# Attention and routed experts on one core: the attention steps written out in a new order of units

## The reference

```python
x = L0_attn_x                                            # (4, 512, 128)
# attention: 16 heads of 8, causal; weights with a LoRA part
qkv = x @ w_attn.T + b_attn + 0.5 * (x @ la.T @ lb.T)
att = softmax(where(causal, q @ k.T / sqrt(8), -inf))
y   = lora_linear(att @ v, w_proj, b_proj, la_proj, lb_proj)
x   = layernorm(x + y)
# experts: 8 experts of width 352, the best two per token
probs = softmax(x @ router_w); w, idx = top_k(probs, 2); w /= sum(w)
x   = layernorm(x + sum_k w_k * (silu(x @ gate[idx_k]) * (x @ up[idx_k])) @ down[idx_k])
```

## Time and profile before

| | us |
|---|---|
| runs | 396.70, 397.21, 397.75 |
| profiled execution, its own time | 399.86 |
| span in that profile | 398.0 |
| start-up, to the first score for a row max | 0 to 34 |
| maxima of groups 0 and 1, then PE idle | 34 to 66.7 |
| attention steps 0 to 15 | 66.7 to 241.2 |
| last batch's rows, scatters, tables | 241.5 to 273.8 |
| experts (39 tiles) | 273.8 to 368 |
| gathering, second normalising, store | 368 to 398 |

### The profile page before, as it was taken

How to read it: one execution, slowest core, us unless ns; L and a number is a source line. 1 busy time by engine, 2 the same in 40 slices (tenths; PEclk the granted TensorE clock), 3 DMA queues, 4 the chain that set the end, 5 groups by cost and what they waited for, 6 DMA issues and landing times.

```text
span 398.0 us, 7773 instructions
## 1 busy us (share of the span) xinstructions
PE 276.3 (69%) x2334; PEld 155.7 (39%) x2335; DVE 215.8 (54%) x551; ACT 156.8 (39%) x258; POOL 158.9 (40%) x273
## 2 busy tenths in 40 slices
PE   3984602969787888788878774305999999999200
PEld 2542201323243334333334222203777777877100
DVE  1489901647578677887786002441655555555082
ACT  1371002647465477547654361110333233333014
POOL 8047100323325386448644700270233343444262
PEclk9996555689899699989996898555999999999755
DMA  6199998754500000000000100042021111110253
GB/s 155 48 232 193 358 202 274 193 78 77 86 3 3 9 30 23 3 0 30 30 3 1 50 8 0 0 155 60 25 60 53 48 48 48 53 49 28 84 145 103
DMA packets 36107, 30.31 MB, mean 76 GB/s; under 512 B 4130, under 2 KB 33989, under 8 KB 36054
## 3 DMA queue, kind: packets, MB, share of 16 engines
q1 hardware_dynamic: 27710, 20.59, 21.9%
q10 hardware_dynamic: 6000, 5.07, 5.3%
q0 software_dynamic: 2368, 4.27, 3.2%
HBM read 16.86 MB, written 13.09 MB: 75 GB/s over the span
## 4 chain that ended last, share of the span: by engine, by line
PE 45%; issue 10%; DVE 10%; POOL 8%; DMA 8%; ACTq 7%; ACT 6%; SPq 3%; another core or an unknown queue 2%; POOLq 1%; DVEq 0%
PE slot L1260 12%; PE pvo L1274 7%; ACTq L673 6%; PE pvo L1089 5%; DMA Qs<-mT 4%; PE slot L1266 3%; PE slot L1068 3%; ACT Pt L655 3%; POOL rows_scratch L527 3%; POOL Pt L503 2%; PE slot L1049 2%; SPq L352 2%; PE misc L1097 1%; PE misc L1253 1%
## 5 line engine op out<-in xcount | busy, mean ns | idle before, releaser
L788 DVE TENSOR_REDUCE negm<-slot 128x2 f32<-128x1024 f32 (+2 forms) x96 | 97.5, 1040 | 54.5 <-PE slot L1049 53.4
L655 ACT ACTIVATE Pt<-slot 128x1024 f32<-128x1024 f32 (+1 forms) x96 | 83.8, 881 | 72.6 <-PE slot L1068 64.5
L503 POOL TENSOR_SCALAR_AFFINE_SELECT Pt<-Pt 128x512 f32<-128x512 f32 x56 | 35.8, 639 | 88.2 <-ACT Pt L655 67.0
L571 POOL DMA_INDIRECT chosen_scratch<-Pt x39 | 38.3, 983 | 65.7 <-ACT Pt L713 64.4
L1068 PE MATMUL slot<-Qs,Ks 51*128 51x512 bf16 (+3 forms) x256 | 37.4, 331 | 31.5 <-DMA Qs<-mT 22.8
L1089 PE MATMUL pvo<-Pt,V 128*9 128x128 f32 (+3 forms) x512 | 55.6, 498 | 0.9 <-issue 0.9
L1260 PE MATMUL slot<-GUW,Pt 128*128 x156 | 55.0, 476 | 0.0
L942 DVE COPY Pt<-slot 128x256 f32<-128x256 f32 x39 | 16.6, 425 | 42.7 <-PE slot L1266 24.2
L1049 PE MATMUL slot<-Ks,Qs 48*128 48x512 bf16 (+3 forms) x256 | 39.0, 345 | 0.0
L527 POOL DMA_INDIRECT rows_scratch<-early,place x32 | 31.8, 994 | 15.4 <-issue 8.3
L1274 PE MATMUL pvo<-DW,Pt 128*128 (+1 forms) x234 | 33.4, 278 | 1.2 <-ACT Pt L713 0.7
(11 more groups left out here) (165 smaller groups left out, 373.6 us busy)
## 6 DMA issues: line engine op xcount, KB each, us to landing
Qs<-parts_scratch SPq DMA_DIRECT2D x8, 384.0 KB, 6.9
Ks<-parts_scratch SPq DMA_DIRECT2D x8, 384.0 KB, 9.4
Pt<-rows_scratch SPq DMA_DIRECT2D x39, 65.0 KB, 1.7
Qs<-chosen_scratch SPq DMA_DIRECT2D x8, 256.0 KB, 5.0
parts_scratch<-Pt SPq DMA_DIRECT2D x4, 384.0 KB, 5.5
parts_scratch<-early SPq DMA_DIRECT2D x4, 384.0 KB, 3.5
GUW<-in_L_ffn_gate_proj_dram ACTq DMA_DIRECT2D x1, 1408.0 KB, 16.6
GUW<-in_L_ffn_up_proj_dram ACTq DMA_DIRECT2D x1, 1408.0 KB, 18.1
```

The lines of the kernel that those rows point to most:

```text
L503: pool.affine_select(out=v, in_=v, compare_op=ALU.is_ge, fill=0.0, base=0, pattern=[[0, HQ], [1, P]], channel_multiplier=-1).then_inc(sele ...
L571: pool.indirect_dma_start(chosen_scratch, bass.IndirectOffsetOnAxis(xg[:, ring, C:C + 1].bitcast(U32), 0), ys[:, ring % OUT_RING, :], None ...
L655: act.activation(p_view(par, kb)[:, h0:h0 + heads, :].rearrange("p (c a) q -> p a c q", a=2), t_view(u, (2 * u + 1) % 3), ACT.Exp, scale=S ...
L788: dve.tensor_reduce(negm[:, par, qb, h0:h0 + heads].rearrange("p (c a) -> p a c", a=2), s_view(u, n), AX_X, ALU.max, negate=True).then_inc ...
```

## The change

The order of work on each engine is written out step by step, with the same arithmetic:

- the loops over the batches on DVE, ACT and POOL are gone, as are the semaphores that count inside them;
- PE's units come as q0 k0 q1 k1 q2 q3 k2 q4 k3 k4 k5 q5, with new slots to match, and the four groups of values of a step are placed anew;
- the maxima of a group are laid out so that one transpose of 48 columns does for four, and two DMAs for four bring them to the stacks;
- the end of a batch is spread over three steps: k = 1 (y, projection, residual, statistics, normalised rows), k = 2 (x1, router, choice), k = 3 (count, places);
- the normalised rows are made by ACT, as x times the inverse deviation plus a shift that DVE forms;
- POOL's scatters are at other places: the first at the end of step k = 3, three in the next step, four in the one after, three of these behind its last select;
- the expert weights are loaded by SyncE, one expert behind the maxima of each of groups 4 to 11.

```diff
-            def store_maxrows(g, par):
+            def store_maxrows(g):
 
                 sp.wait_ge(mT_copied, g + 1)
-                for h in range(HQ):
-                    row = HALF * (h % 2) + ROWS
-                    sp.dma_start(Qs[row:row + PARTS, bass.ds(g, 1), h // 2, :],
-                                 mT[PARTS * h:PARTS * (h + 1), par, :]).then_inc(maxrows[par], 16)
+                for a in range(2):
+                    row = HALF * a + ROWS
+                    n = MAX_ROWS // 2
+                    sp.dma_start(Qs[row:row + PARTS, g].rearrange("e c (t q) -> e (c t) q", q=P),
+                                 mT[n * a:n * (a + 1), g % 2, :]).then_inc(maxrows[g % 2], 16)
+
+            def load_expert(e):
+                for w, src in enumerate((gate_proj, up_proj)):
+                    sp.dma_start(GUW[:, e, w, :], src[e]).then_inc(experts_loaded, 16)
+                full = F // P
+                sp.dma_start(DW[:, e, 0:full, :], down_proj[e, 0:full * P, :].rearrange("(k p) c -> p k c", p=P)).then_inc(experts_loaded, 16)
+                sp.dma_start(DW[0:F - full * P, e, full, :], down_proj[e, full * P:F, :]).then_inc(experts_loaded, 16)
...
-            with sp.Fori(2, G // 2) as pair:
-                store_maxrows(2 * pair, 0)
-                store_maxrows(2 * pair + 1, 1)
+            for g in range(4, G):
+                store_maxrows(g)
+                if g < 4 + E:
+                    load_expert(g - 4)
...
+            def first_step(g):
+                b = g // 4 - 2
+                if b >= 0:
+                    scatter_rows(b, 1)
+                select(g, 0)
+                if b >= 0:
+                    scatter_rows(b, 2)
+                select(g, 1)
+                if b >= 0:
+                    scatter_rows(b, 3)
+                select(g, 2)
+                split_max(g + 2)
+                select(g, 3)
+
+            def second_step(g):
+                b = g // 4 - 2
+                if b >= 0:
+                    scatter_rows(b, 4)
+                select(g, 0)
+                if g >= 4:
+                    inverse_deviation(g // 4 - 1)
+                select(g, 1)
+                select(g, 2)
+                split_max(g + 2)
+                select(g, 3)
+                if b >= 0:
+                    for n in range(5, 2 * TB):
+                        scatter_rows(b, n)
+                if g >= 4:
+                    number_rows(g // 4 - 1)
...
+            def normed(b):
+                act.wait_ge(shift1_ready, b + 1)
+
+                act.wait_ge(scattered, 16 + 2 * TB * 16 * b)
+                for t in range(TB):
+                    last = act.activation(rows[:, 0, t, 0:C], XR[:, t, :], ACT.Identity, bias=shift1[:, t:t + 1], scale=rstd[:, t:t + 1])
+                last.then_inc(x1_ready, 1)
...
+            def step(g):
+                k, b = g % 4, g // 4 - 1
+                if k == 1 and b >= 0:
+                    copy_yT(b)
+                exp(g, 0)
+                if k == 2 and b >= 0:
+                    copy_x1(b)
+                exp(g, 1)
+                if g >= 1:
+                    copy_pv(g - 1)
+                if g + 1 < G:
+                    copy_mT(g + 1)
+                exp(g, 2)
+                if k == 2 and b >= 0:
+                    copy_scores(b)
+                exp(g, 3)
+                exp(g, 4)
+                exp(g, 5)
+                if k == 1 and b >= 0:
+                    normed(b)
+                if k == 2 and b >= 0:
+                    exp_gap(b)
...
+            def step(g):
+                k, b, scores = g % 4, g // 4 - 1, g + 2 < G
                 for u in range(NU):
+                    if u == NU - 1 and g >= 1:
+                        if k == 2 and b >= 0:
+                            choose(b)
+                        normalize(g - 1)
+                        if k == 1 and b >= 0:
+                            shift_mean(b)
                     if scores:
-                        row_max(g + 2, par, u, (2 * u) % 3)
+                        row_max(g + 2, u)
+                    if u == 2 and k == 1 and b >= 0:
+                        residual(b)
+                    if u == 3 and k == 1 and b >= 0:
+                        deviations(b)
+                    if u == 1 and k == 3 and b >= 0:
+                        place_rows(b)
...
+                scores_q(g + 2, 1)
+                if k == 2 and ended:
+                    pe.wait_ge(y_done, g - 1)
+                    transpose_x1(b)
...
+                pe.wait_ge(max_done, NU * (g + 2) + 2)
+                scores_q(g + 2, 3)
...
+                transpose_max(g + 1)
+                pe.wait_ge(exp_done, NU * g + 2)
+                scores_k(g, 2)
+                pe.wait_ge(max_done, NU * (g + 2) + 3)
+                scores_q(g + 2, 4)
+                if k == 2 and ended:
+                    pe.wait_ge(mT_copied, g + 2)
+                    route(b)
```

More of the change, by code:

```diff
@@ L527, in scatter_rows @@
                 pool.indirect_dma_start(rows_scratch, bass.IndirectOffsetOnAxis(place[:, j, t:t + 1], 0),
                                         rows[:, j, t, :], None).then_inc(scattered, 16)
-            def step(g, k, end=None, chosen_before=None, scores=True):
-                selects = not isinstance(g, int) or g < MASKED_FROM
-                par = k % 2
-                if end is not None:
-                    inverse_deviation(end)
-                for kb in range(TB):
-                    if selects:
-                        select(g, par, kb)
-                    if kb == 1 and end is not None:
-                        number_rows(end)
-                    if kb == TB - 1 and scores:
-                        split_max(g + 2, par)
-                    if chosen_before is not None:
-                        scatter_rows(chosen_before, k, kb)
@@ new lines, in third_step, with fourth_step @@
+            def third_step(g):
+                select(g, 0)
+                select(g, 1)
+                select(g, 2)
+                split_max(g + 2)
+                select(g, 3)
+            def fourth_step(g):
+                select(g, 0)
+                select(g, 1)
+                select(g, 2)
+                split_max(g + 2)
+                select(g, 3)
+                if g >= 4:
+                    scatter_rows(g // 4 - 1, 0)
+            split_max(0)
+            split_max(1)
@@ L562, in _ @@
+            pool.wait_ge(v_out, B)
+            for b in range(B):
+                first_step(4 * b)
+                second_step(4 * b + 1)
+                if b < B - 1:
+                    third_step(4 * b + 2)
+                    fourth_step(4 * b + 3)
+            for n in range(2 * TB):
+                scatter_rows(B - 2, n)
             inverse_deviation(B - 1)
             number_rows(B - 1)
[L564 to L566 removed]
+            for n in range(2 * TB):
+                scatter_rows(B - 1, n)
@@ L681, in _ @@
             act.wait_ge(v_full, B)
-            step(0, 2, pv=False)
-            step(1, 3)
-            with act.Fori(0, B - 1) as b:
-                for k in range(4):
-                    step(4 * b + 2 + k, k, end=b)
-            step(G - 2, 0)
-            step(G - 1, 1, maxrows=False)
+            for g in range(G):
+                step(g)
             copy_pv(G - 1)
             copy_yT(B - 1)
+            normed(B - 1)
             copy_x1(B - 1)
@@ L882, in _ @@
             for g in range(2):
                 for u in range(NU):
-                    row_max(g, g, u, (NU * g + u) % 3)
-            step(0, 2, pv=False)
+                    row_max(g, u)
+            step(0)
             for s in range(2):
                 dve.wait_ge(parts_stored[s][B - 1], 16 * PARTS)
-            step(1, 3)
+            for g in range(1, 4):
+                step(g)
             dve.wait_ge(xb_ready, 1)
             dve.wait_ge(lists_ready, 1)
-            with dve.Fori(0, B - 1) as b:
-                loop[0] = b
-                chain[0] = 0
-                for k in range(4):
-                    step(4 * b + 2 + k, k, end=b)
-                assert chain[0] == LINKS, chain[0]
@@ L898, in _ @@
-            loop[0] = None
-            chain[0] = LINKS * (B - 1)
-            step(G - 2, 0, scores=False)
-            step(G - 1, 1, scores=False)
-            normalize(G - 1, 3)
+            for g in range(4, G):
+                step(g)
+            normalize(G - 1)
             residual(B - 1)
-            normed(B - 1)
+            deviations(B - 1)
+            shift_mean(B - 1)
             choose(B - 1)
```

388 lines of the change are left out of this document (186 added, 202 removed).

## The result

The changed kernel takes 385.56 us (median of four runs, 380.72 to 387.76) where the kernel before, run beside it, took 397.48 (396.7 to 399.49): a ratio of 0.965, 95% interval 0.955 to 0.975. Ratios are formed from the runs near the fastest of their kernel, and so can differ a little from the ratio of the two medians. The forecast was 380.5 with a range of 365 to 392. The profiled execution took 386.17 us with a span of 383.9, so 14.1 us less than the 398.0 of before.

A forecast was written before the change was run, and what follows sets the result against it. Attention bounds the answer: a 17.4 us PE hole waiting for maxima, then slot waits with no engine full. -16.2 - 2.3 - 11.3 - 4.9 + 17.0 + 1.0 = -16.7 from 397.2 gives 380.5 us, range 365 to 392.

The forecast's parts named there:

- Expert loads on SyncE, start: Start of attention: ACT copies the maxima earlier, so PE goes on at 50.5 instead of 66.7 us, -16.2 us.
- signs of right (50 to 52) and wrong (after 55): Start of attention: first exp at 50 to 52 us would confirm the forecast, one after 55 us would refute it.
- time of the parts: Start, SyncE's queue: without expert data, batch 1's parts are written at 39 to 40 us and its stacks issued by 41.
- third rival: SyncE's queue: expert loads hold up the maxima of eight groups, making the kernel slower, 420 us at 15 us a load; chance 0.04.
- First four steps: Attention's opening steps: maxima of groups 2 and 4 still queue behind a stack load; 37.5 us instead of 39.8, -2.3.
- New order, steps 4 to 13: Middle of attention: PE's new unit sequence and placed extras take 98.5 us instead of 109.8, -11.3 us.
- plain step: Attention step without projection or routing: 8.3 us (8.0 to 8.9) by the slot walk, instead of 8.7.
- Rival 2: Attention steps: the order gives nothing, steps stay 8.7 us and the extras as large; 391.8 us, chance 0.10.
- Scatter wait: Steps 9 and 13: ACT's normalised rows wait for the previous batch's scatters, 7.0 us without PE work, 8.5 each, +17.0 us.
- Rival 1: Steps 9 and 13: waiting for the scatters costs nothing, as they come early enough or land faster; 363.5 us, chance 0.13.
- Last two steps: End of attention: ACT's 6.4 us stop goes with the unrolled loop, batch 2's extras come; 20.0 us for 24.9, -4.9.
- Tail: After attention: batch 3's normalising on ACT takes 1.9 us instead of 1.13 on DVE, plus a shift product; +1.0 us.

The follow-up runs named there:

- second buffer: The changed kernel with two row buffers and two tables of places used in turn by the batches, no scatter moved: 356.82 us, ratio 0.901.
- quarters: The changed kernel with the stacks of batches 2 and 3 loaded in four pieces each behind stores of maxima, expert loads at groups 8 to 15: 373.35 us, ratio 0.953.
- maxima before the stack: The changed kernel with the store of group 0's maxima issued ahead of the load of batch 1's stacks: 382.41 us, ratio 0.971.
- after again: The changed kernel itself run once more, nothing altered: 384.51 us, ratio 0.964.
- old unit order: The changed kernel with PE's units again as q0 k0 q1 k1 to q5 k5 and the slots of before: 388.38 us, ratio 0.980.
- scatters forward: The changed kernel with POOL's scatters of batches 0 and 1 moved earlier, none behind the second step's last select: 366.33 us, ratio 0.921.
- queue in the order of need: The changed kernel with two row buffers, SyncE's stores and loads reordered by when they are needed, and Y in its own memory: 357.68 us, ratio 0.897.
- held kernel run again: Second run of the changed kernel with batch 2's eight scatters held until all weighted values are done: 377.34 us, ratio 0.945.

## Why the prediction was right, and where not

The forecast's span was 381.3, the measured 383.9, and the 2.6 us between them are the sum of larger misses: start +3.4, first four steps +0.4, steps 4 to 13 -8.8, last two +7.4, tail +0.8, the rest -0.6. That the total came so close is luck: the two largest misses cancel.

**Expert loads on SyncE, start: mechanism right, size wrong.** -12.8 instead of -16.2; the first exp came at 54.71, between the signs of right (50 to 52) and wrong (after 55). The step that failed is the time of the parts. The text puts them at "39 to 40", and the sum then counts from a first stack issue at 37 to 38, which can't come before them; from 39 to 40 it would have given 51.6 to 52.6. SyncE got the parts at 41.65 (before: 45.24), though the load on the DMA engines did fall as assumed (the same stretch, before first, then after; columns as above, the second last is the DMA share):

```profile
33.00:43.50 10.50, 6.24 (x59) 2.54 (x58) 10.43 (x15) 0.00 (x0) 4.30 (x9) 0.50 1.07 251
```

```profile
33.00:43.50 10.50, 6.17 (x58) 2.53 (x58) 10.43 (x16) 0.00 (x0) 4.31 (x9) 0.50 0.56 175
```

With the engines half free (share 0.56) the last of these stores still landed 12.63 us after its issue began; the slowest took 13.6 us to land where before it took 16.0, and SyncE needed 7.08 us to issue the six instead of 8.94. So sharing was only a part of why the parts were late; what holds them besides is open. The other number of this term, 12.6 us from the first stack issue to the maxima behind it, held: 41.65 to 53.93 is 12.3. The loads in their new place hold up no maxima, as assumed, and the third rival is out: the kernel before with them alone took 386.21 us. That they cost nothing at all isn't shown, since that kernel gave back 3 to 4 of the 14.5 us won at its start. The edit gave 10 to 11.5 us alone: it took 25.46 us of issuing off the engine on which the first step waited.

**First four steps: right.** 37.9 for 37.5; the stops for the maxima of groups 2 and 4 stand where the rows put them.

**New order, steps 4 to 13: two terms mis-sized.** Expected were 98.5 us and 17.0 for the waits, 115.5; it took 106.7. The plain step is 8.5 to 8.9 us, not 8.3. The steps with extra work are shorter than the walk gave: between the copies of maxima 5 and 15, without the waits, the steps lie at 8.3 to 11.0 us, and the ten of them take 92.4 (second buffer) where the kernel before took 109.6. But the unit order isn't what did this. Put back, it cost 5.4 us there and 3 to 6 in all. So the larger part of these 17 us, some 12, came with the rest of the rewrite: one transpose for the maxima, normalised rows on ACT, and the places of the extra work. Which of these isn't separated. The clearest sign is the distance between the copies of maxima 6 and 7: 14.07 us before and 8.49 after. Rival 2 had the plain step nearly right and the steps with extra work wrong.

**Scatter wait: right.** 7.56 and 7.54 us of idle time ahead of ACT's rows, where the working gave 7.0; the last scatter lands 2.28 us after its start, where the earlier trace rows gave 2.32. With what follows, the waits cost 15.5 to 15.8 us in the traces by two cures, 17.0 expected. So all that follows the 15.1 us of idle time, the half clock among it, cost 0.4 to 0.7 us for both, where 3.0 had been put in. (The granted clock of each profile is only ever 0.50 or 1.00; a figure between them, as 0.52 in step 14 and 0.83 in step 10, is the mean of a stretch.) Rival 1 is out: in the present order nothing hid it.

**Last two steps: the reason failed.** 27.4 us for 20.0. The stop was put down to the end of the loop over the batches. Unrolled, it is still there (3.29 and 2.38 us), so the end of a loop isn't its cause. What the runs showed in its place is a row of eight scatters beside every such stop, and no stop where the row was held; in three profiles the row stands without a stop, so what sets it off is open. No loop is left in this place in the kernel after, and no instruction packet lies in the stretch. With the scatters held the last stretch is 6.5 us shorter in the pair run side by side (13.8 for 20.3) and 8.4 against the profile of after (22.2): 19 to 21 us for the two steps, so the 20.0 would have been about right without the stop.

**Tail: the number near, the reason wrong.** 34.4 us from the last copy of weighted values to the experts, 32.6 before: +1.8 for +1.0 (34.2 and 32.4 if one ends at the experts' first product, as for the kernels that follow). It was put down to ACT's normalised rows. But the three kernels that have these rows and no stop (quarters, maxima before the stack, second buffer) take 32.4 to 32.6 us, and the five that have both (after, after again, old unit order, scatters forward, queue in the order of need) 34.1 to 34.4. So the rows cost nothing that shows, and the 1.7 us are the stop's. In the kernel after the granted clock is 0.50 from the start of this stretch on; in the kernel with the quarters it is 0.99 over its first 6 us, and the eight products of the projection take 1.16 us there and 2.09 here.

## What to carry to other kernels

Look for what stands ahead of a small transfer in its queue, and put the queue in the order in which things are needed; 12 KB behind a stack load landed 8.8 us after their issue, and behind twelve stores of parts PE waited 9.2 us for them. A buffer that is read by a late DMA is a wait for whoever writes it next: find the last issue, add its landing, and either move the issues forward or give a second buffer; here either took off 15 us. And when an early hole is closed, ask what it had covered: the first attempt at the start won 6.5 us and lost them all one step later. Last, look at the terms of a forecast that came true: here the total was good while four of its terms weren't.

## What was not expected of the hardware

Eight indirect DMAs in a row, 1.27 us apart, went with stops of 3.3 to 6.4 us in ACT's and PE's work in six of ten profiles, and there was none in the four in which they were held; in the kernel after TensorE is at half clock (0.50) for 41 us, 222.6 to 263.5, and as long in four others of the six (31 us in the kernel before), against 34 us, 222.0 to 256.2, in the held kernel run again, where it falls 6 us after the last weighted values and not before them. After the scatter wait of 7.5 us with little work on PE, the granted clock was 0.52 over the next 14.00 us, behind the first one 0.83 over 10.70. The same kernel before took 392.27 us as a median beside one group and 398.8 beside another, so that differences under 6 us between groups say nothing.
